# A one-core image kernel: convolutions one block earlier, a casting load for the stencil matrices, halves in another order, one scalar column in the step's clip, the last chunk in two halves

## The reference, cut to what matters

```python
x = _L0_conv_ref(x, ...)   # patch attention, window attention over x as one row of 16384: x @ Wv_w, then @ Wout_w (64 MB each)
x = _L1_conv_ref(x, ...)   # conv3x3(16->16) -> relu -> conv3x3 -> + x
x = _L2_conv_ref(x, ...)   # the same again
x = _L3_conv_ref(x, ...)   # ten explicit steps of a curvature flow
# one step of _L3_conv_ref
ux, uy, uxx, uxy, uyy = clip(sobel derivatives of u, -10, 10)
K = clip((uxx * uyy - uxy * uxy) / (denK * denK + EPS), -5.0, 5.0)
H = clip(((1 + uy * uy) * uxx - 2 * ux * uy * uxy + (1 + ux * ux) * uyy) / (2 * denH ** 3 + EPS), -5.0, 5.0)
u = u + DT * clip(alpha * K + beta * H, -1.0, 1.0)
u = pad(u[:, :, 1:-1, 1:-1], mode='edge')
...
return 0.7 * u + 0.3 * x
```

## Time and profile before

| | |
|---|---|
| median of 3 runs | 809.05 us (807.56 to 810.9) |
| the profiled execution | 807.85 us, of which the span from first to last instruction 806.1 us |
| TensorE busy | 663.1 us (82%) |
| VectorE busy | 472.7 us (59%) |
| ScalarE busy | 391.0 us (49%) |
| GpSimd busy | 272.6 us (34%) |
| mean granted TensorE clock | 0.95 |
| HBM read | 164.99 MB |

### The profile page before, as it was taken

One profiled execution on the slowest core, in us unless ns is written; L12 is line 12 of the kernel. 1 busy time (PEld: TensorE's weight loads), 2 busy tenths in 40 slices (PEclk: granted clock), 3 DMA queues, 4 the chain that ended last, 5 costly groups with the idle time before them and its releaser, 6 DMA issues.

```text
span 806.1 us, 11634 instructions
## 1 busy us (share of the span) xinstructions
PE 663.1 (82%) x4616; PEld 485.3 (60%) x4616; DVE 472.7 (59%) x669; ACT 391.0 (49%) x653; POOL 272.6 (34%) x239
## 2 busy tenths in 40 slices
PE   0799989799754658898898988898898998998983
PEld 0587735454322226575577876777776776776770
DVE  6840001930300112232235699999999999999996
ACT  1300000500000001120132599999999999999995
POOL 1000000000220500000001567767767667667662
PEclk9999999899978689899999999999999999999997
DMA  9959898998999999999960000000000000000001
GB/s 382 412 187 412 351 433 353 394 437 372 418 384 418 420 419 438 429 427 436 417 268 0 1 2 0 0 0 0 0 0 0 1 0 0 0 0 0 0 0 52
DMA packets 10993, 166.53 MB, mean 207 GB/s; under 512 B 1232, under 2 KB 1360, under 8 KB 5712
## 3 DMA queue, kind: packets, MB, share of 16 engines
q1 hardware_dynamic: 9744, 164.30, 48.7%
q10 hardware_dynamic: 672, 1.41, 0.5%
q0 software_dynamic: 544, 0.33, 0.1%
HBM read 164.99 MB, written 1.05 MB: 206 GB/s over the span
## 4 chain that ended last, share of the span: by engine, by line
PE 30%; DMA 24%; ACT 22%; DVE 17%; issue 6%; POOL 1%; DVEq 0%; ACTq 0%; POOLq 0%; SPq 0%
DMA ring<-wout_w 17%; PE bank L370 7%; PE bank L382 7%; DMA ring<-wv_w 4%; PE bank L556 4%; PE bank L420 4%; PE bank L477 3%; ACT ring L1004 3%; ACT ring L1000 3%; DVE ring L830 2%; DVE ring L817 2%; ACT ring L999 2%; ACT bank L991 2%; ACT ring L1017 2%; DVE reg_b L851 2%
## 5 line engine op out<-in xcount | busy, mean ns | idle before, releaser
L556 PE MATMUL bank<-u_parts,vmr 128*128 128x480 f32 x1360 | 305.6, 382 | 38.3 <-DVE ring L830 37.4
L556 PEld LDWEIGHTS bank<-u_parts,vmr 128*128 128x128 f32 x1360 | 252.4, 188 | 91.5 <-DVE ring L830 52.6
L382 PE MATMUL bank<-ring,small 128*32 128x256 f32 x1152 | 81.5, 446 | 32.1 <-DMA ring<-wout_w 32.1
L1101 POOL TENSOR_TENSOR ring<-ring 128x480 f32<-128x480 f32 x40 | 49.1, 1228 | 99.3 <-DVE reg_a L860 77.1
L382 PEld LDWEIGHTS bank<-ring,small 128*32 128x32 f32 x1152 | 40.7, 128 | 68.7 <-DMA ring<-wout_w 35.6
L794 DVE STREAM_TRANSPOSE reg_b<-bank 128x256 f32<-128x256 f32 x16 | 7.2, 450 | 108.6 <-PE bank L382 108.6
L946 ACT ACTIVATE reg_e<-xa 32x384 f32<-32x384 f32 (+9 forms) x16 | 8.3, 521 | 109.8 <-DVE xa L797 83.4
L370 PE MATMUL bank<-reg_a,ring 128*128 128x256 f32 x256 | 58.0, 389 | 3.6 <-ACT reg_a L904 3.6
L370 PEld LDWEIGHTS bank<-reg_a,ring 128*128 128x128 f32 x256 | 49.9, 196 | 11.3 <-issue 4.3
L382 PE MATMUL bank<-ring,reg_e 128*32 128x256 f32 x512 | 37.1, 457 | 22.7 <-DMA ring<-wv_w 22.7
L1085 POOL CAST vmr<-ring 128x3328 fp32r<-128x3328 f32 x1 | 3.0, 2956 | 149.3 <-DMA ring<-edge 149.3
(11 more groups left out here) (190 smaller groups left out, 1029.0 us busy)
## 6 DMA issues: line engine op xcount, KB each, us to landing
ring<-wv_w SPq DMA_DIRECT2D x16, 4096.0 KB, 26.2
ring<-wout_w SPq DMA_DIRECT2D x15, 4096.0 KB, 34.4
ring<-wqk_p SPq DMA_DIRECT2D x2, 4096.0 KB, 30.5
ring<-wqk_w SPq DMA_DIRECT2D x2, 4096.0 KB, 14.0
ring<-wv_p SPq DMA_DIRECT2D x1, 4096.0 KB, 13.2
ring<-wout_p SPq DMA_DIRECT2D x1, 4096.0 KB, 21.1
ring<-wout_w SPq DMA_DIRECT2D x4, 1024.0 KB, 30.7
ring<-vmats SPq DMA_DIRECT2D x1, 1664.0 KB, 6.2
```

The costliest lines, as they stand in the source:

```text
L382: ins = te.matmul(bank[32 * j:32 * j + 32, b_, n0:n0 + 256], lhs(c), slot[k % NSLOT][:, c, 256 * j:256 * j + 256], start=start and c == 0, ...
L556: last = te.matmul(dst[:, 0:NF], mat(m, first), p3[:, 2 + off:S + off, :], start=(high and n == 0), stop=(not high and n == len(terms) - 1))
L1101: p.tensor_tensor(abs_[n], ab[n][:, 0:NF], ab[n][:, NF:2 * NF], ALU.add).then_inc(po["absum"], 1)
```

## The change: what it does

1. `convs_after`: layers 0 and 1 of waves 0 to 2 now both stand behind the wave's last block, layers 2 and 3 behind the next two. Behind blocks 6, 10 and 14 stands no layer any more. Wave 3 is as it was.
2. The left half is regrouped behind block 14, ahead of block 15's products; chunk 3's part uses bank 0.
3. `vmats` goes from HBM into `vmr` by a transfer on POOL's queue, which casts on its way; the buffer `vm` and the cast L1085 are gone.
4. The split of u's left half and border (`FIRST`, 272 columns) is made by ACT (`hi_first`) and POOL (`lo_first`) during the last layer, that of the right half (`SECOND`, 272 columns) when it is there. Half 1 is regrouped chunk by chunk, not in two passes over all chunks.
5. The clip: `min(dif - mid, DT)`, then `max(., -DT) + u`: one column and two immediates where three columns were.
6. The end: no pad for the last three slots and the last chunk; the products read only the 30 inner columns, small VectorE instructions on 2 x 16 elements write the edge columns; the last chunk is done in two halves of 240 columns with a transfer each.

The diff's core:

```diff
-    return [(w, s - G + 1 - G * w) for w in range(WAVES - 1) if 0 <= s - G + 1 - G * w < NCONV]
+    return [(w, layer) for w in range(WAVES - 1) for layer in range(NCONV) if s == G * (w + 1) - 1 + max(layer - 1, 0)]
...
+def parts(x):
+    return [(2, S)] if x < NCH - 1 else [(2, S // 2 + 1), (S // 2 + 1, S)]
+def chunk_bank(x, half):
+    return 4 + x if half or x < NCH - 1 else 0
...
# SP
-            sp.dma_start(vm, vmats).then_inc(ld_vm, 16)
-            sp.dma_start(edge_m, edge).then_inc(ld_vm, 16)
+            sp.dma_start(edge_m, edge).then_inc(ld_edge, 16)
...
# TensorE
-                if s_ == NO - 1:
+                if s_ == NO - 2:
...
-                        te.wait_ge(ve["bank_turn"], NO + x + 1)
+                        te.wait_ge(ve["bank_turn"], NO + min(x, 2) + 1)
...
+                    if (w, layer) == (WAVES - 1, 0):
+                        te.wait_ge(ac["u_in"], NCH)
...
-            for h in range(2):
-                te.wait_ge(ve["conv"], pairs_done(WAVES - 1, NCONV - 1, h))
-                for x in range(NCH):
-                    for g in (2 * h, 2 * h + 1):
-                        ins = chunk_rows(x, g, 1)
-                    if h:
-                        ins.then_inc(pe["chunk"], 1)
+            te.wait_ge(ve["bank_turn"], NO + NSLOT)
+            for x in range(NCH):
+                for g in range(G):
+                    if x == 0 and g % 2 == 0:
+                        te.wait_ge(ve["conv"], pairs_done(WAVES - 1, NCONV - 1, g // 2))
+                    ins = chunk_rows(x, g, 1)
+                ins.then_inc(pe["chunk"], 1)
...
-            te.wait_ge(po["vm"], 1)
-            te.wait_ge(ld_vm, 32)
+            te.wait_ge(ld_vm, 16)
+            te.wait_ge(ac["hi_first"], NCH)
+            te.wait_ge(po["lo_first"], NCH)
...
-                te.wait_ge(ac["pad"], SLOTS - NCH + x + 1)
-                te.matmul(bank[:, EDGE_BANK[x], :], edge_m, u_in(x), start=True, stop=True).then_inc(pe["edge"], 1)
+                te.wait_ge(ve["u"], SLOTS - NCH + x + 1)
+                for n, (a_, b_) in enumerate(parts(x)):
+                    te.matmul(bank[:, EDGE_BANK[x] + n, 0:(b_ - a_) * B], edge_m, u[x][:, a_ * B:b_ * B],
+                              start=True, stop=True).then_inc(pe["edge"], 1)
...
# VectorE
-                v.tensor_scalar(dif, dif, high_lim, low_lim, ALU.min, ALU.max).then_inc(ve["clipd"], 1)
+                v.tensor_scalar(dif, dif, mid, DT, ALU.subtract, ALU.min).then_inc(ve["clipd"], 1)
...
-                v.scalar_tensor_tensor(inner, dif, mid, inner, ALU.subtract, ALU.add).then_inc(ve["u"], 1)
+                v.scalar_tensor_tensor(inner, dif, -DT, inner, ALU.max, ALU.add).then_inc(ve["u"], 1)
...
# ACT
+                if (w, layer) == (WAVES - 1, NCONV - 1):
+                    a.wait_ge(pe["slot_used"], U_ALL)
+                    a.wait_ge(ac["u_in"], NCH)
+                    for x in range(NCH):
+                        a.activation(u_hi[x][:, FIRST], u[x][:, FIRST], ACT.Copy).then_inc(ac["hi_first"], 1)
...
# POOL
-            p.wait_ge(ld_vm, 32)
-            p.tensor_copy(vmr[:, :], vm).then_inc(po["vm"], 1)
+            p.wait_ge(pe["slot_used"], U_ALL)
+            p.dma_start(vmr[:, :], vmats).then_inc(ld_vm, 16)
+            p.wait_ge(ac["hi_first"], NCH)
+            p.wait_ge(ac["halo"], 2 * WAVES * NCONV)
+            p.wait_ge(ve["halo"], 4 * WAVES * NCONV)
+            for x in range(NCH):
+                p.tensor_tensor(u_lo[x][:, FIRST], u[x][:, FIRST], u_hi[x][:, FIRST].bitcast(F32),
+                                ALU.subtract).then_inc(po["lo_first"], 1)
```

More of the change, by code:

```diff
@@ L184, in build @@
         dt_ab, five_ab, ten_ab = (sm(2) for _ in range(3))
-        neg_b, mid, low_lim, high_lim = (sm(1) for _ in range(4))
+        neg_b, mid = (sm(1) for _ in range(2))
         wft = sm(KC * 2 * B)
@@ L884, in _ @@
                 for x in finished[k - SLOTS] if k >= SLOTS else ():
[L886 to L889 removed]
+                    finish(x)
         @block.scalar
@@ L945, in _ @@
                 a_, b_ = columns(w, layer)
-                halo_rows(a, lambda o, i: a.activation(o, i, ACT.Copy), (0,), w, layer, halo_source(layer),
-                          halo_waits(w, layer), ac["halo"])
                 if (w, layer) == (WAVES - 1, 0):
@@ L994, in slot_step @@
                     high(k + 2, c, not first or k + 2 > NCH)
-                elif k > 2:
-                    pad(k - 2, (k - 3) % NCH)
                 if old:
@@ L1037, in _ @@
                 slot_step(k, k % 2, k <= SLOTS, True, None)
-            pad(SLOTS, NCH - 1)
         @block.gpsimd
```

48 lines of the change are left out of this document (30 added, 18 removed).

## The result

The changed kernel takes 799.44 us (median of 4 runs, 797.88 to 801.35); the kernel before, run beside it, takes 809.47 (807.56 to 810.9). The ratio is 0.9879, with a 95% interval of 0.9846 to 0.9911. The profiled execution took 798.39 us, its span 796.6, against 807.85 and 806.1 before. The forecast was 800.6 for the median and 799.4 for the profiled execution. The forecast gain was 8.45 us; the profiled executions lie 9.46 apart, the medians 10.03.

What follows compares the result with a forecast made beforehand. Loads set the pace up to block 15, then an uncovered chain, then VectorE's loop with ACT close behind. Gains 1.1 + 1.75 + 1.1 + 4.0 + 0.5 = 8.45 took 809.05 to 800.6 us (median), range 797.0 to 805.0.

Steps and rivals of the forecast that it cites:

- A: Block 15 to wave 3: the last piece's landing sets wave 3's start; gain 1.1 us, bounds 0 and 2.8.
- D: Loop's clip: fewer scalar columns shorten each slot by 0.11 us over 36 slots; gain 4.0 us, bounds 0 and 5.3.
- B: Wave 3: without POOL's cast, VectorE's L84 copies are no longer held and L508 isn't late; gain 1.75 us, or 0.
- C: Stencils' start: halved ACT and POOL splits and chunk-by-chunk order start TensorE earlier; gain 1.1 us, bounds 0.4 and 1.8.
- E: Kernel's end: no pad wait, fewer columns, smaller last instruction, halved transfer perhaps nothing; gain 0.5 us, bounds 0.2 and 0.9.
- R1: Loop: ACT or both engines' chains hold the slot at 8.60, all of D lost; 804.6 us, chance 0.12.
- R2: Seam at wave 3: pauses make TensorE's clock fall; 802.3 us, or 809.8 if it stays low; chance 0.12.
- R3: Ahead of the first stencil: casting transfer lands late, beyond its 24 us; slower from 32 us on; chance 0.03.
- R4: Early layers don't help: A gives nothing, C's halves only trade places; 802.8 us; chance 0.11 together with mixtures.

Runs made afterwards that it cites:

- the best version: Changed kernel with 0.3 x copies ahead of the loop, chunk 0 split before chunk 2's copy, first stencil awaiting chunk 0 alone: 797.32 us.
- The clip alone: Kernel before with only the clip changed to one scalar column and two immediates (part 5): 804.07 us, ratio 0.9936.
- the split alone: Kernel before with only part 4, u's split in two halves and the right half regrouped chunk by chunk: 808.33 us.
- the third away: Changed kernel with the last scalar column, L870's, replaced by the immediate 0.01, another limit than the reference's: 798.08 us.
- the end alone: Kernel before with only part 6: no last pads, products on 480 columns, last chunk in two halves: 808.63 us.
- the layers put back: Changed kernel with the layers of waves 0 to 2 again one behind each of four blocks: 800.38 us.
- the old order put back: Changed kernel with the right half regrouped in two passes over all four chunks, as before: 798.3 us.
- POOL kept busy: Changed kernel with a POOL copy of the cast's size (3328 columns) put beside wave 3: 801.36 us.
- the head alone: Kernel before with only parts 1 and 2, layers drawn forward and left half regrouped behind block 14: 808.41 us.

## Why the prediction was right, step by step

The mechanisms held for what the change gives, and the sum of 8.45 stands against 9.46 in the profiled execution. All five terms have the right sign and place. Four came out larger than forecast and one smaller. Of the 1.01 between the sums, 0.5 is the luck of an earlier landing (A). One figure beside the sum does not come out: the range's lower end, "D at its upper end and A at 2.8", is 1.3 and 1.7 below 800.6, which is 797.6 and not 797.0.

**A: right in kind, 1.1 against 1.43.** The last piece set the changed kernel's seam as forecast, block 15 began at 409.95 ("by about 410"), and the last quarter began at the landing. Of the 1.43, 0.9 to 1.0 is the head's; the rest is the landing, 413.6 for 414.1, which also moves in kernels that don't touch it. What the prediction says of the kernel before, that only what stands behind the last piece counts, was not so there: TensorE's 12.82 us from block 14 on counted whole. The sum took the measured 417.02 as its start, so this did not reach the number. One size on the way was wrong: block 12 began 5.0 later than before, not 2 to 3 (389.74 for 384.79), since block 11 behind a wait of 6.06 took 6.49 us. It was made good by block 14 all the same (404.74 for 404.20), and SP's issues of the last pieces, 1.8 later, starved nothing.

**B: 1.75 against 1.99.** The wait of 1.75 counts from the end of the products ahead of it. Where nothing waits, the next ones begin before that end: of the changed kernel's timeline, L521 starts at 423.25, 0.16 ahead of L516's end (419.88 plus 3.53), and its eight products take 1.25 instead of 1.33. Together that is the missing 0.24.

**C: 1.1 against 0.83.** The order gave 0.37, as said. The halves gave 0.46 where 0.7 was counted. The term that was most off is ACT's half: TensorE begins 0.83 us behind ACT's split, and before it was 0.84 (442.29 less 441.45,'s L978), though the instruction is half as long. What held it was another wait, `ve["u_in"]` at 2, for VectorE's copy of chunk 3's right half (L891 now, L874 before). TensorE's first stencil starts 0.25 to 0.27 us behind that copy's end in thirteen of the fourteen traces, 438.52 for 438.26 in the changed kernel, while ACT's split of chunk 0 ends at 438.11 there. The fourteenth is the best version, which does not wait for it at that place and starts 0.54 ahead of its end. The profile's [0.72 <-ACT u_parts L1012] names the split of chunk 1, which ends last but which the first stencil does not need. And the high products, 0.88 for four, now last longer than POOL's half, so of POOL's 1.32 us between the first high and the first low product 0.44 go, where 0.6 less 0.1 was counted.

**D: 4.0 against 4.29.** A column costs 59 to 61 ns, between the two rows' 55 and 74; VectorE became 0.119 shorter and the slot 0.111, which is the very number taken; it was picked between 0.09 and 0.13, so that it is exact is luck. 36 slots make 4.0; the rest of stage D is its first slot, 8.57 for 8.92, a slot that the prediction left out with the first four. The clip alone makes it 8.81 and the split alone 8.70, so about 0.1 of it is the clip's and 0.2 is part 4's, which C did not count. The Trainium skill ("VectorE: DVE Perf Modes", The TRN2 errata) gives (N + 151) / 0.96 ns for an fp32 `tensor_tensor` add, 657 at 480 elements; it does not give it for `scalar_tensor_tensor`, to which the prediction carried it over. The 659 measured for the instruction without a column agrees. The reason given for taking 0.11 and not 0.13, that ACT sets a second limit, is borne out: the columns give 65, 46 and 32 ns in turn, and with the third away ACT's chain holds every second slot.

**E: 0.5 against 0.96, the term that was mis-sized most.** To the last finishing instruction it is 0.63, inside the bounds; 0.06 of it is the clip's, since the stretch starts with the last change of u (0.66 for 0.72), and the end alone gives 0.57. The halved transfer was put at "perhaps nothing" and gives 0.33: 128 KB land in 1.7 us, 256 KB in 2.0. The rows of before held only transfers of 256 KB, and I took no slope from the larger ones.

**The rivals.** R1 (8.60 stays) fell to the clip alone. R2 did not happen at its place: behind the wait for the last piece (0.90 to 1.39) and the one of 0.90 the clock stayed at 1.00, in all eight kernels with the new head. But the reason given against it, that waits of under 2 us leave the clock alone, is refuted: behind pauses of 1.68 and 1.92 in wave 3 it fell in two other kernels (last section). R3 was far off: the transfer landed 7.3 us after its issue, of the 24 us that it had; the Trainium skill's fit ("DMA: Bandwidth & Descriptors", Anatomy of one DMA) gave 5.9, and the measurement is 1.4 above it. R4 fell to the layers put back and, for C, to the old order put back, which left the halves' 0.46.

## What to carry to other kernels

At the end of a streamed load, look first whether the engine waits for the last piece at all. If it doesn't, all its work since its last wait counts; take work out of that row until it waits, and from there only what stands behind the last piece counts. Read starts against the landing, not against the clock of one execution. On an engine that is busy all through a loop, a per-partition scalar operand that could be an immediate is worth removing, at 60 ns each here, until the next engine's chain is met. A long instruction of GpSimd can hold a copy of VectorE that starts beside it until it ends, so a conversion was cheaper here on the way in.

## What the runs showed of the hardware that was not expected

**The cast's price depended on TensorE's clock.** With the pause of 1.60 to 1.92 us that POOL causes in wave 3, the next 24 products took 3.85 us in four traces (the end alone and POOL kept busy, pause 1.60 in each; the kernel before, 1.75; the head alone, 1.86) and 5.5 at a granted clock of 0.68 or 0.69 in two (the split alone, 1.68; the clip alone, 1.92). The pauses' lengths do not sort them: 1.68 is below 1.75 and 1.86. So the same stall costs 1.8 to 2.1 us in stage B, or 3.6 to 3.8. I found nothing in the traces that tells beforehand which it will be, and leave it open.

**The casting transfer is nearly as fast as the plain one.** 1664 KB landed in 7.3 us on POOL's queue with the cast (7.2 to 7.6 in the nine traces that have it), in 6.2 on SP's queue without it. How much of the 1.1 is the cast's and how much the queue's is not shown.
